# Linear attention: two rounded units pass ahead of the pair's and output weights in the queue's program

## What is computed

```python
def step(state, blk):                     # 32 heads of 64, blocks of tokens
    qi, ki, vi = blk
    aw = jnp.einsum('bhid,bhjd->bhij', qi, ki) * dd
    intra = jnp.einsum('bhij,bhjd->bhid', aw, vi)
    inter = jnp.einsum('bhid,bhde->bhie', qi * qd_, state)
    new_state = state * bd_ + jnp.einsum('bhsd,bhse->bhde', ki * kd_, vi)
    return (new_state, intra + inter)
...
gate = jax.nn.sigmoid(hidden_states @ gate_w.T)
return gate * attn @ out_w.T

def _mx_dequant(t):                       # layer 1's feed-forward, gate, up and down weights
    max_abs = jnp.max(jnp.abs(blocks), axis=-1)
    scales = jnp.maximum(max_abs / _FP8_MAX, _EPS)
    q = (blocks / scales[..., None]).astype(jnp.float8_e4m3fn).astype(jnp.float32)
    return (q * scales[..., None]).reshape(rows, feat)
```

## Time and profile before

| | us |
|---|---|
| median of 3 runs | 1886.53 |
| the runs | 1886.53, 1886.53, 1880.79 |
| profiled execution, its time | 1877.34 |
| its span | 1875.5 |
| mean granted TensorE clock in the span | 0.997 |
| linear attention's rounds, from the span's start | about 839 to 1366 |

### The profile page before, as it was taken

The page is one execution under the profiler, slowest core; times in us unless marked ns, Lnnn a source line. Parts: engine busy times, 40 slices in busy tenths (PEclk is TensorE's granted clock), DMA queues, the critical chain, the costliest instruction groups (busy, mean ns, idle before and its releaser), DMA issues. The chain is left out here.

```text
span 1875.5 us, 24735 instructions
## 1 busy us (share of the span) xinstructions
PE 1826.5 (97%) x9384; PEld 1377.2 (73%) x9388; DVE 1229.1 (66%) x2114; ACT 713.6 (38%) x1151; POOL 376.8 (20%) x286
## 2 busy tenths in 40 slices
PE   8999999999999999999999999999999999999998
PEld 6888786444444688578888888887888866888886
DVE  6435665666754766686777777777782367766666
ACT  4312233455454688434333333332344432322211
POOL 0000011112100588401111111211210001243532
PEclk9999999999999999999999999999999999999999
DMA  6102233233314111242314214214212110110101
GB/s 225 46 1 73 90 74 70 65 77 72 102 26 135 47 59 66 78 130 64 93 29 142 84 40 138 88 40 138 78 40 77 69 45 23 46 45 25 44 1 45
DMA packets 109049, 132.67 MB, mean 71 GB/s; under 512 B 36066, under 2 KB 72930, under 8 KB 107394
## 3 DMA queue, kind: packets, MB, share of 16 engines
q1 hardware_dynamic: 108932, 131.10, 22.8%
HBM read 97.27 MB, written 14.75 MB: 60 GB/s over the span
## 5 line engine op out<-in xcount | busy, mean ns | idle before, releaser
L858 DVE TENSOR_REDUCE b_nm<-ps 128x1 f32<-128x1024 f32 x128 | 152.3, 1219 | 59.3 <-PE ps L846 58.7
L1222 ACT ACTIVATE b_pr<-ps 128x512 f32<-128x512 f32 x256 | 133.8, 601 | 117.1 <-PE ps L1086 116.7
L253 PE MATMUL ps<-d_x_high,d_w_high 128*128 128x512 f32 x384 | 154.4, 402 | 1.7 <-issue 1.7
L255 PE MATMUL ps<-d_x_high,d_w_low 128*128 128x512 f32 x384 | 149.8, 390 | 0.0
L254 PE MATMUL ps<-d_x_low,d_w_high 128*128 128x512 f32 x384 | 149.7, 390 | 0.0
L2489 POOL TENSOR_TENSOR d_sqsum<-d_sqsum,d_sq 128x512 f32<-128x512 f32 x32 | 46.0, 1439 | 471.7 <-ACT d_sq L2400 471.5
L1100 PE MATMUL ps<-b_pr,b_VS 128*64 128x512 f32 x512 | 123.8, 605 | 0.0
L1812 POOL TENSOR_TENSOR c_h<-c_h,c_w_row 128x512 f32<-128x512 f32 x64 | 105.6, 1658 | 29.5 <-DVE c_h L1827 20.3
L1086 PEld LDWEIGHTS ps<-b_qS,b_kS 98*128 98x128 f32 x256 | 43.1, 188 | 66.7 <-issue 47.9
L1086 PE MATMUL ps<-b_qS,b_kS 98*128 98x512 f32 x256 | 89.9, 432 | 1.8 <-ACT b_pr L1222 1.7
L846 PE MATMUL ps<-b_kS,b_qS 96*128 96x512 f32 x256 | 83.3, 409 | 3.5 <-DVE b_nm L858 2.3
(11 more groups left out here) (466 smaller groups left out, 4966.5 us busy)
## 6 DMA issues: line engine op xcount, KB each, us to landing
b_kS<-b_k_parts SPq DMA_DIRECT2D x96, 128.0 KB, 2.3
f_rows<-d_fw SPq DMA_DIRECT2D x24, 512.0 KB, 2.9
f_w<-f_rows SPq DMA_DIRECT2D x12, 1024.0 KB, 4.8
c_w_row<-w_rows SPq DMA_DIRECT2D x16, 512.0 KB, 3.5
b_qS<-b_q_parts SPq DMA_DIRECT2D x96, 64.0 KB, 2.0
d_w<-in_d_wq SPq DMA_DIRECT2D x16, 256.0 KB, 2.8
d_w<-in_d_wk SPq DMA_DIRECT2D x16, 256.0 KB, 3.0
d_w<-in_d_wg SPq DMA_DIRECT2D x16, 256.0 KB, 3.4
```

Source lines behind the costliest of these rows:

```text
L253: nc.tensor.matmul(out, lhsT[0], rhs[0], start=start, stop=False)
L255: return nc.tensor.matmul(out, lhsT[1], rhs[0], start=False, stop=stop)
L858: nc.vector.tensor_reduce(nm[:, g % 2, u:u + 1], c.ps[:, banks:banks + 2, :], AX.XY, ALU.max, negate=True).then_inc(job_read, 1)
L1222: nc.scalar.activation(pr[:, n % RING, :], c.ps[:, 4 + n % BANKS, :], ACT.Exp).then_inc(exp_done, 1)
```

## The change

In SP's passes 6, 10 and 14 (p % 4 == 2 and p > 4) the first two of the three units are stored, and the next two raw ones loaded, at the head of the pass, ahead of the pair's weights and of the output weights. The third stays where it was. No transfer is added or taken away, and no other engine's program changes.

```diff
+    def pass_unit(sp, u):
+        store_rounded(sp, u)
+        if u + FSLOTS < FUNITS:
+            sp.wait_ge(stored_f[u % FSLOTS], 16 * (u // FSLOTS + 1))
+            load_raw(sp, u + FSLOTS)
+
...
             for p in range(PAIRS):
+                stored = units_rounded(p - 3) if p >= 2 else 0
+                if p % GP == GP - 2 and p > GP:
+                    for u in range(stored, stored + UNITS_GROUP):
+                        pass_unit(sp, u)
+                    stored += UNITS_GROUP
                 pair_weights(sp, p)
                 if p % SG == 0 and p > SG:
                     output_weights(sp, p // SG - 1)
...
                 if p >= 2:
-                    for u in range(units_rounded(p - 3), units_rounded(p - 2)):
-                        store_rounded(sp, u)
-                        if u + FSLOTS < FUNITS:
-                            sp.wait_ge(stored_f[u % FSLOTS], 16 * (u // FSLOTS + 1))
-                            load_raw(sp, u + FSLOTS)
+                    for u in range(stored, units_rounded(p - 2)):
+                        pass_unit(sp, u)
```

## The result

The changed kernel takes 1870.85 us (median of 5 runs, 1870.21 to 1875.37), the kernel before 1883.46 (5 runs, 1880.66 to 1886.53). The ratio is 0.9945 with an interval of 0.9928 to 0.9963: faster by 0.55%. The forecast was 1879.6 us with a range of 1873.7 to 1886.5.

A forecast was written before the change was run, and what follows sets the result against it. TensorE, busy for 97% of the span, was taken to bound the kernel. The terms, 6.12 + 0.96 - 0.16 = 6.9 us, taken from the shown median of 1886.53 gave 1879.6 us, range 1873.7 to 1886.5.

The forecast's parts named there:

- What bounds, and why the states were late: TensorE bounds; it waits 4.4 us (round 12, states) and 0.9 (round 4, mask products) because unit stores stand behind output weights.
- Terms 1, 2 and 3: Round 12's wait and slow clock go, 6.12 us; round 4's wait goes, 0.96; new wait at `products(13, 1)` costs 0.16.
- Terms 4 and 5: In SP's queue: the pair's weights moving back, and the same transfers moved to another stretch, each cost nothing.
- term 5: In SP's queue: same transfers and bytes, only moved, cost nothing; at worst one DVE wait for a unit, 5.13 us.
- the step from the profiled execution to the others: Whole kernel: the shown median's 9.2 us above the profiled execution is carried over, so the gain comes off 1886.53 us.
- theory 1: Posed after the result: the profiled execution was a cheap one; in others the same waits cost more through TensorE's slow clock.
- Theory 2: Posed after the result: waits always cost what the profile shows; the rest comes from passes 6 and 10 or pair's weights.
- Theory 3: Posed after the result: the gain beyond what the profiles show is scatter of a few executions.
- Rival A: Before round 13's mask products POOL blocks DVE, 1.08 us a hit; two hits leave a gain of 4.7 us, chance 0.15.

The follow-up runs named there:

- e7: Changed kernel with the two units ahead of the output weights only, behind the pair's weights; ratio 0.9955 to the kernel before, median 1873.52 us.
- e8: Changed kernel with the third unit (20) also ahead of the weights in pass 14; ratio 1.0021 to the kernel before.
- e11: The kernel before, unchanged, profiled once more; one execution, 1880.8 us.
- e2: Kernel before with only pass 14's two units moved ahead, passes 6 and 10 as before; ratio 0.9968 to the kernel before.
- e3: Kernel before with only passes 6 and 10's units moved ahead, pass 14 as before; ratio 0.9992 to the kernel before.
- e4: Changed kernel with DVE's third part of rounding put ahead of the states in round 12; ratio 0.9994 to the kernel before.
- e12: Changed kernel with DVE's third rounding part ahead of the states in round 12, profiled once more; one execution, 1876.4 us.
- e6: Changed kernel with only the two stores ahead, the two raw loads behind output weights, mask and decays; ratio 0.9990 to the kernel before.
- e10: The kernel before, unchanged, run a third time for one more profile; ratio 0.9998 to the kernel before.
- e9: The changed kernel, unaltered, measured a third time; ratio 0.9967 to the kernel before, median 1873.48 us of 10 runs.

## Why the prediction was right and where it was wrong

**What bounds, and why the states were late: right.** All four profiles of the kernel before show the two waits, and with both taken away no wait of TensorE for DVE in rounds 1 to 14 is above 0.3 us. (The prediction says "in the 16 rounds", but its rows end at 1341: a third wait for DVE, of 0.56 us in round 15, stands in every profile, before and after. It costs the sum nothing.)

**Terms 1, 2 and 3 as they stand in that profile: right.** The stage from `products(1, 0)` to `products(14, 0)` is 6.55 us shorter between the two profiles, the forecast's sum 6.9. The new wait is 0.25 for 0.16 (0.26 and 0.27 in the others). That nothing else would come behind it was 0.5 us off, the stretch with the wait for ACT, 19.99 for 19.48. The span without its clock part fell by 5.0 us in the mean of the executions; the sum without its clock part was 5.25.

**Terms 4 and 5 at nothing: right.** e7 shows that the weights' new place costs nothing that can be told, e8 that there is an end to the cover. For term 5, no wait of DVE for a unit is left in the changed profile.

**Where it failed, first: the step from the profiled execution to the others.** "I carry the difference over", the prediction said of the 9.2 us between the profiled execution and the median of three. That median was high: 102 executions have a mean of 1881.4, 5 us below it, and some reach 1876.4. A gain of 6.9 from the mean is 1874.5. The range had the same fault: its low end was the fastest of three runs less the gain, and the fastest of three is no low end. Of the 8.8 us between forecast and measured median this is 5.1; 1.5 are what the gain was put too low (8.4 for 6.9, below), and 2.1 are that the median of the first five executions lies under the mean of all 21, which is scatter.

**Second: two terms were sized from one execution, and others pay more.** The forecast took 1.67 us of slow clock in round 12 and 0.96 us in round 4 as fixed. In the mean of the executions the whole clock part is 3.4 us (9.44 less 6.06). Round 4's wait is 0.89 to 0.96 in three of the four profiles of the kernel before and 2.21 in the fourth (e11) and in e2, and once, in e11, 1.7 us of clock came with it. The clock's shortfall at the long wait is 1.7 in three profiles and 3.4 in e11, and 3.4 in each of the three others with a wait of that length (e3, e4, e12). Part of the 3.4 falls into the wait itself, so TensorE's own step grew by only 0.7 us (42.08 for 41.36). In e11 the stage costs 9.8 us more than in the changed kernel's first profile, in the three cheap ones 6.3 to 6.7. So theory 1 holds in kind, but more by the short wait than by the long one that it named, and with POOL's hits on DVE beside the clock. Theory 2 falls: the waits' price differs between profiles of one kernel, and the parts alone give 6.0 and 1.5 us, together no more than the whole. Theory 3 is a good part of it: the first comparison (0.9945, 10.4 us) and the second (0.9948) show more than the 8.4 us of all executions, the third (0.9967) less.

**Rival A**, POOL in DVE's way, did not come ahead of the mask products in the changed kernel, where POOL was held up instead, but it made e6's second wait and lengthens round 4's. Its upper bound of two hits was too low: four were seen.

**What stays open.** The profiles give a mean difference of 458.6 - 451.5 = 7.1 us for the stage, the executions 8.4 with an interval of 7.2 to 9.5. The 7.1 lies just below the interval, and four profiles and three are few. Whether the 1.3 between them is more of the dear executions than one in four, or losses of clock in other stages that fell on the kernel before by chance, was not settled. In the profiles such losses are no more frequent before: 3.4 us near 615 stand in every profile, and beyond that the four of the kernel before show 1.7 near 190 (e10), the three of the changed one 1.7 near 310 and 1.7 near 330 (e9).

## What to carry to other kernels

In a queue that issues in program order, look for a transfer that is free to go behind a wait that is met much later: here the buffer was ready 35 us before its store was issued, and the cost was not the transfer but the wait that it caused on DVE and, through DVE, on TensorE. When moving it ahead, move it only past waits that are met later than its own; one unit more, whose data came 30 us later, turned 8 us of gain into 4 of loss. And price a wait of TensorE from several executions: the profile shows one, and the clock behind the wait and the number of times that POOL held DVE up are not the same in the next. Anchor the time on many runs, not on three.

## What the runs showed of the hardware

At waits of TensorE of 4.39, 4.39 and 4.40 us the granted clock fell short of full by 1.7 us in all, at 4.44, 4.45, 4.65, 4.84 and 5.17 (e6) by 3.4, and at 9.43 by 5.1, at half of full (1.2 GHz) in the windows that lie wholly in it. Part of the larger losses lies inside the wait and costs nothing. A wait of 2.21 us came with 1.7 in one profile (e11) and with nothing in another (e2), one of 1.05 with nothing (e6). All of these losses are 1.7 us, two times or three times 1.7.

DVE's operations with two SBUF inputs and POOL's took turns in e6, each of POOL's four holding DVE for 1.08 us, and in the changed kernel POOL's two sums took 5.65 us beside DVE's operations, which kept their time. By the rule of the Trainium skill, "SBUF — State Buffer" (section "SBUF: two separate sides"), whoever starts first holds the pair for the whole instruction; the rows agree on the blocking, but 5.65 us for two sums that take 3.33 elsewhere suggest that POOL did not get its turn after the one instruction that it met. What decides between the two cases was not tested.
